# Second layer norm applied behind the adapter product, with a centred adapter: a Hyena block with an adapter on one Trainium2 core

## The reference, cut to what matters

```python
# x: (8, 2048, 512); D_MODEL 512, ORDER 2
def _layernorm(x, eps=1e-5):
    m = mean(x, -1); v = var(x, -1)
    return (x - m) / sqrt(v + eps)

def hyena(x):                                   # only the last branch survives the loop
    proj = (x @ in_proj_w + in_proj_b).reshape(B, L, C, 3)
    v = short_conv3(proj[..., 0]) + short_b
    h = coefs(pos)[:, :, 1]                     # small network over positions
    conv = irfft(rfft(v, n=2 * L) * rfft(h, n=2 * L))[:, :L]
    return (proj[..., 2] * conv) @ out_w + out_b

def adapter(x):                                 # K = 8 chosen of 32 adapters
    out = einsum('k,kod,bsd->bso', weights, W[ids], x)
    return out + einsum('k,ko->o', weights, b[ids])

x = x + hyena(_layernorm(x))
x = x + adapter(_layernorm(x))                  # the layer norm that the change is about
```

## Time and profile before

| | |
|---|---|
| median of 3 runs | 2428.93 us (2424.77, 2428.93, 2429.24) |
| the profiled execution's own time | 2427.41 us |
| its span, first to last instruction | 2425.2 us |
| mean granted TensorE clock | 0.979 |
| TensorE busy, whole span | 2317.4 us, 96% |
| VectorE busy | 1553.6 us, 64% |
| GpSimd busy | 942.7 us, 39% |
| ScalarE busy | 843.5 us, 35% |

### The profile page before, as it was taken

How to read it: one execution, slowest core, us unless ns; L and a number is a source line. 1 busy time by engine, 2 the same in 40 slices (tenths; PEclk the granted TensorE clock), 3 DMA queues, 4 the chain that set the end, 5 groups by cost and what they waited for, 6 DMA issues and landing times. The chain is left out here.

```text
span 2425.2 us, 39710 instructions
## 1 busy us (share of the span) xinstructions
PE 2317.4 (96%) x12804; PEld 1602.1 (66%) x12804; DVE 1553.6 (64%) x2188; ACT 843.5 (35%) x1151; POOL 942.7 (39%) x1189
## 2 busy tenths in 40 slices
PE   6779999999999999779999988999999999999998
PEld 2257777777777777534444435777777777777776
DVE  5834444343434444257777767888888888888886
ACT  3334444444444444334444441222222222222222
POOL 1322222222222222100000006777777777777774
PEclk9879999999999999889999998999999999999999
DMA  5534545445444546489999988766666556665653
GB/s 184 217 100 139 186 165 178 160 154 196 156 160 145 190 153 212 158 337 356 361 355 358 359 315 257 227 182 177 179 177 181 174 175 179 175 176 177 179 179 103
DMA packets 180517, 496.60 MB, mean 205 GB/s; under 512 B 19419, under 2 KB 19740, under 8 KB 159332
## 3 DMA queue, kind: packets, MB, share of 16 engines
q1 hardware_dynamic: 150756, 395.10, 50.7%
q10 hardware_dynamic: 29696, 100.68, 11.5%
HBM read 276.27 MB, written 219.43 MB: 204 GB/s over the span
## 5 line engine op out<-in xcount | busy, mean ns | idle before, releaser
L1055 DVE TENSOR_TENSOR m_m<-m_psA,m_spec 128x1024 f32<-128x1024 f32 x256 | 295.4, 1216 | 132.0 <-PE m_psA L960 128.6
L709 POOL TENSOR_TENSOR vl<-v,vh 128x512 fp32r<-128x512 f32 x128 | 165.2, 1291 | 390.0 <-ACT vh L663 390.0
L1222 ACT ACTIVATE b_zh<-b_psT 128x512 fp32r<-128x512 f32 x128 | 76.5, 597 | 636.8 <-PE b_psT L1271 636.8
L977 PE MATMUL m_psW<-m_m,mats 64*64 64x512 f32 x2048 | 249.6, 593 | 0.0
L960 PE MATMUL m_psA<-m_xin,mats 64*64 64x512 f32 x1536 | 203.9, 602 | 30.5 <-DMA m_xin<-spec_f 13.5
L181 PE MATMUL psV<-wvh,nth 128*128 128x512 f32 x512 | 213.6, 417 | 0.6 <-DVE ntl L791 0.6
L810 DVE TENSOR_TENSOR gto<-psG,bgr 128x512 f32<-128x512 f32 x128 | 87.7, 685 | 195.5 <-PE psG L183 195.4
L181 PE MATMUL b_psO<-woh,b_oh 128*128 128x512 f32 x512 | 211.2, 412 | 0.0
L181 PE MATMUL b_psF<-wfh,b_zh 128*128 128x512 f32 x512 | 207.6, 406 | 2.8 <-DVE b_zl L1324 2.8
L1191 POOL TENSOR_TENSOR b_corr<-b_edge,b_v 128x512 f32<-128x512 f32 x128 | 199.2, 1556 | 14.5 <-DMA b_edge<-edge_f 14.4
L182 PE MATMUL b_psF<-wfl,b_zh 128*128 128x512 f32 x512 | 201.3, 393 | 0.0
(11 more groups left out here) (122 smaller groups left out, 4494.6 us busy)
## 6 DMA issues: line engine op xcount, KB each, us to landing
spec<-fs1o SPq DMA_DIRECT2D x64, 1024.0 KB, 8.8
spec<-m_wo ACTq DMA_DIRECT2D x64, 1024.0 KB, 8.4
b_fin<-spec SPq DMA_DIRECT2D x128, 512.0 KB, 4.6
m_xin<-spec SPq DMA_DIRECT2D x31, 2048.0 KB, 11.8
xg<-in_L_attn_x_dram SPq DMA_DIRECT2D x64, 512.0 KB, 6.1
gate_d<-gto SPq DMA_DIRECT2D x32, 1024.0 KB, 3.9
b_gin<-gate_d SPq DMA_DIRECT2D x128, 256.0 KB, 3.6
b_xin<-in_L_attn_x_dram SPq DMA_DIRECT2D x256, 128.0 KB, 3.2
```

The source lines that it names most:

```text
L709: pool.tensor_tensor(vl[:, t % 2], v[:, t % 2], vh[:, t % 2].bitcast(F32), ALU.subtract).then_inc(v_lo, 1)
L977: mm = pe.matmul(psW[pair % 2][half[slot], q, :], ws[slot][half[q]], m[half[q], pair % RM, part, slot, :], start=part == 0, stop=part == 1)
L1055: dve.tensor_tensor(m[:, (k - 2) % RM, part], psA[k % RA][:], spec[:, par, part], ALU.mult).then_inc(m_done, 1)
```

## The change

The second layer norm is no longer applied to y ahead of the product.

- In `front`, a new VectorE stage `level` takes the mean of each row of the mixed adapter off it, one of four pieces in each of four rounds of the last batch, ahead of the write to HBM. `store_mix` moves from tile 5 to tile 11 of the last batch in SP's list and also waits for `level`.
- In `back`, `norm` is gone, `turn_z` transposes y itself, and `scalars` computes only r (two operations instead of four). `finish` multiplies the product by r and adds `b_yb` in one operation, and waits for r.
- `z_high`, `z_low`, `turn_z`, `adapt`, `finish` and `store` run with a lag one smaller, and on VectorE `finish` stands ahead of `z_low` and `o_low`.

```diff
 (front, SP)
-                    if isinstance(b, int) and b == B - 1 and t == MIX:
+                    if isinstance(b, int) and b == B - 1 and t == T - 5:
                         sp.wait_ge(ad_used, MIX * B)
+                        sp.wait_ge(ad_level, CT)
                         sp.dma_start(ad_mix, ad_sum[:]).then_inc(ad_stored, 16)
                         sp.dma_start(ad_bias, adb_sum[:]).then_inc(ad_stored, 16)
 (front, VectorE)
-                pipelined(dve, B, T, [(nt_low, 3), (v_bias, 4), (moments, 0), (g_bias, 4), (mix, 9)])
+                def level(b, t):
+
+                    if not (isinstance(b, int) and b == B - 1 and MIX <= t < MIX + CT):
+                        return
+                    k = t - MIX
+                    dve.wait_ge(ad_used, MIX * (B - 1) + k + 1)
+                    dve.bn_stats(ad_stats[:, k], ad_sum[:, k]).then_inc(ad_step, 1)
+                    dve.wait_ge(ad_step, 2 * k + 1)
+                    dve.bn_aggr(ad_mean[:, k], ad_stats[:, k]).then_inc(ad_step, 1)
+                    dve.wait_ge(ad_step, 2 * k + 2)
+                    dve.tensor_scalar(ad_sum[:, k], ad_sum[:, k], ad_mean[:, k, 0:1], None, ALU.subtract).then_inc(ad_level, 1)
+
+                pipelined(dve, B, T, [(nt_low, 3), (v_bias, 4), (moments, 0), (g_bias, 4), (mix, 9), (level, 9)])
 (back, GpSimd)
                     if old(b, t, 2):
-                        pool.wait_ge(z_done, no(b, t) - 1)
-                    r, m = rstd[:, t % 2:t % 2 + 1], shift[:, t % 2:t % 2 + 1]
+                        pool.wait_ge(res_done, no(b, t) - 1)
+                    r = rstd[:, t % 2:t % 2 + 1]
                     pool.tensor_tensor(r, mv[:, 1:2], eps[:], ALU.add).then_inc(pow_step, 1)
-                    pool.tensor_tensor(m, mv[:, 0:1], minus[:], ALU.mult).then_inc(pow_step, 1)
-                    pool.wait_ge(pow_step, 3 * no(b, t) + 2)
-                    pool.tensor_tensor(r, r, power[:], ALU.pow).then_inc(pow_step, 1)
-                    pool.wait_ge(pow_step, 3 * no(b, t) + 3)
-                    pool.tensor_tensor(m, m, r, ALU.mult).then_inc(norm_ready, 1)
+                    pool.wait_ge(pow_step, no(b, t) + 1)
+                    pool.tensor_tensor(r, r, power[:], ALU.pow).then_inc(norm_ready, 1)
 (back, ScalarE)
-                def norm(b, t):
-                    ...
-                pipelined(act, B, T, [(z_high, 4), (o_high, 1), (norm, 3), (store, 6)])
+                pipelined(act, B, T, [(z_high, 3), (o_high, 1), (store, 5)])
 (back, TensorE)
                 def turn_z(b, t):
-                    pe.wait_ge(z_done, no(b, t) + 1)
+                    pe.wait_ge(y_done, no(b, t) + 1)
                     if old(b, t, 1):
                         pe.wait_ge(z_lo, no(b, t))
                     for ct in range(CT):
-                        mm = pe.transpose(psT[:, ct * P:(ct + 1) * P], z[:, t % 2, ct * P:(ct + 1) * P], ident[:])
+                        mm = pe.transpose(psT[:, ct * P:(ct + 1) * P], y[:, t % 2, ct * P:(ct + 1) * P], ident[:])
-                pipelined(pe, B, T, [(conv_pair, 0), (adapt, 5), (turn_z, 4), (turn_o, 1), (project, 2)])
+                pipelined(pe, B, T, [(conv_pair, 0), (adapt, 4), (turn_z, 3), (turn_o, 1), (project, 2)])
 (back, VectorE)
-                        dve.wait_ge(z_done, no(b, t) - 1)
+                        dve.wait_ge(t_ps, no(b, t) - 1)
                 def finish(b, t):
                     dve.wait_ge(ff_ps, no(b, t) + 1)
                     dve.wait_ge(yb_done, no(b, t) + 1)
+                    dve.wait_ge(norm_ready, no(b, t) + 1)
-                    dve.tensor_tensor(res[:, t % D], psF[t % 2][:], yb[:, t % D], ALU.add).then_inc(res_done, 1)
+                    dve.scalar_tensor_tensor(res[:, t % D], psF[t % 2][:], rstd[:, t % 2:t % 2 + 1], yb[:, t % D], ALU.mult, ALU.add).then_inc(res_done, 1)
-                pipelined(dve, B, T, [(gate, 1), (residual, 3), (z_low, 4), (o_low, 1), (finish, 5), (bias_x, 0)])
+                pipelined(dve, B, T, [(gate, 1), (residual, 3), (finish, 4), (z_low, 3), (o_low, 1), (bias_x, 0)])
```

More of the change, by code:

```diff
@@ L522, in front @@
             adb_sum = sb("adb_sum", [P, C])
+            ad_stats = sb("ad_stats", [P, CT, 6])
+            ad_mean = sb("ad_mean", [P, CT, 2])
             wgt = sb("wgt", [P, NIDS])
@@ L541, in front @@
             ad_stored = sem("f_ad_stored")
+            ad_step = sem("f_ad_step")
+            ad_level = sem("f_ad_level")
             power_set = sem("f_power_set")
@@ L1084, in back @@
             y = sb("b_y", [P, 2, C])
-            z = sb("b_z", [P, 2, C])
             yb = sb("b_yb", [P, D, C])
@@ L1092, in back @@
             rstd = sb("b_rstd", [P, 2])
-            shift = sb("b_shift", [P, 2])
             power = sb("b_power", [P, 1])
             eps = sb("b_eps", [P, 1])
-            minus = sb("b_minus", [P, 1])
             psC = [ps("b_psC0"), ps("b_psC1")]
@@ L1124, in back @@
             norm_ready = sem("b_norm_ready")
-            z_done = sem("b_z_done")
             yb_done = sem("b_yb_done")
@@ L1167, in _ @@
                 pool.memset(eps[:], EPS).then_inc(power_set, 1)
-                pool.memset(minus[:], -1.0).then_inc(power_set, 1)
-                pool.wait_ge(power_set, 3)
+                pool.wait_ge(power_set, 2)
                 def scalars(b, t):
```

## The result

The changed kernel takes 2447.07 us (median of 4, 2446.04 to 2447.91) against 2426.85 before (median of 4): ratio 1.0088, 95% interval 1.0075 to 1.0101 (the two medians alone give 1.0083). It is some 20 us slower. The forecast was 2426, the range ended at 2440. The profiled execution took 2446.04 us, its span is 2444.2.

The account below looks back on a forecast made before the run. TensorE was taken to bound the back stage, busy 929.74 of 930 us. The terms, 0 steady - 1.7 at the end - 1.1 at the start = -2.8 us from the 2428.93 median, gave 2426 us; range 2422 to 2440.

Parts of the forecast that it names:

- the part on VectorE: Back stage: finish takes 0.06 us more, filling an idle hole; the new wait and 0.74 a round would not bind.
- the steady term of the sum: Back stage's repeated pairs of rounds, 14.81 us each on TensorE: no stall, so 0 us change.
- Does y come in time?: Back stage: y done 5.95 us behind the odd turn, even turn loading at 6.12, so TensorE does not stall.
- Rival 1: Back stage: the y loop outlasts TensorE's pair if GpSimd saves under 0.385 us a round; 2433 to 2439 us, chance 0.20.
- this margin of 0.1 us: Back stage: y's slack ahead of the even turn, 0.17 us, or some 0.12 after the semaphore.
- The saving on GpSimd: Back stage: two of four small operations go, saving 0.41 us a round, bounds 0.28 and 0.5.
- `finish` and the port: Back stage: finish, with one SBUF tensor, stays outside VectorE's port lock with GpSimd and takes a constant 0.68 to 0.74 us.
- Rival 3: Back stage: finish takes the shared port and delays GpSimd; 2451 us, or 2487 if both rounds pay; chance 0.08.
- Front stage: Front stage: level adds 1.8 us in each of four rounds, 7.3 in all, hidden in VectorE's idle time; cost 0.
- The ends: Back stage's ends: one TensorE stand fewer at the end gains 1.7 us, a shorter start gains 1.1.
- The sum of the repaired kernel: Whole kernel: 0 steady, 1.7 and 1.1 us gained at the ends, giving 2426.1 from the median of 2428.93.

Follow-up runs that it names:

- e1: Changed kernel with finish waiting for norm_ready at the last tile alone: 2425.91 us against 2427.6 for the kernel before, ratio 0.9993.
- e2: Changed kernel with 32 semaphore increments more on VectorE ahead of the back stage's loop: 2427.34 us, ratio 1.0001 to the kernel before.
- e7: Changed kernel with an empty stage of lag 5 in VectorE's list, cutting the loop one round later: 2426.48 us, ratio 0.9993 to the kernel before.
- e9: Kernel before with the new front stage alone (level and the later store_mix), its own back stage kept: 2426.74 us, ratio 1.0000.
- e8: Changed kernel with finish waiting at the last tile alone and an empty lag-5 stage on VectorE: 2425.69 us, ratio 0.9993 to the kernel before.
- e3: Kernel before with only the wait for norm_ready added in finish: 2427.73 us, ratio 1.0000.
- e5: Changed kernel with finish waiting at the last tile alone, plus 24 semaphore increments ahead of VectorE's loop: 2449.15 us, ratio 1.0087 to the kernel before.
- e6: Changed kernel with 128 semaphore increments ahead of VectorE's loop: 2451.86 us, ratio 1.0088 to the kernel before.

## Why the prediction was wrong, point by point

**The step that failed** is in the part on VectorE: "The new wait for `norm_ready` is for a value of the round before. If the cover were gone, 0.74 a round on VectorE (83% busy) would still not bind." I costed the wait by whether it would ever have to wait. In the loop it never does, as `bn_aggr` has waited for the same value. Its price is the instruction itself, 14 more in the loop body and 12 ahead of it, and where they put the body's end. The second half of the slip is in the steady term of the sum, put at 0 from one pair of rounds that holds no jump back: the shorter lags took away y's round to spare and moved the jump to a round without a hole. That term measured some 21 us (next paragraph). Without the loads it is 0 even with the shorter lags (e1, e2), and so it is with the loads where the jump stands ahead of an odd round (e7). No rival had any of this; the range left it out.

**What it cost.** Five jumps in the steady loop. The five pairs, by stretch:

```profile
1714.71:1734.44 19.73, 16.61 (x74) 12.23 (x73) 11.48 (x18) 2.22 (x4) 9.70 (x10) 0.91 0.45 133
1838.34:1857.15 18.81, 16.60 (x74) 12.14 (x72) 11.47 (x18) 2.17 (x4) 9.70 (x10) 0.91 0.46 140
1961.10:1979.80 18.70, 16.58 (x74) 12.15 (x73) 11.52 (x18) 2.17 (x4) 9.68 (x10) 0.91 0.45 139
2083.70:2102.60 18.90, 16.61 (x74) 12.15 (x73) 11.53 (x18) 2.17 (x4) 9.71 (x10) 0.91 0.44 137
2206.50:2223.60 17.10, 15.06 (x74) 11.01 (x73) 11.55 (x18) 2.18 (x4) 9.69 (x10) 1.00 0.49 154
```

Together 93.24 us instead of 5 x 14.81 = 74.05: 19.2 us too many. TensorE stands for 93.24 - 81.46 = 11.8 of them, 3.1 us in the first pair and 2.0 to 2.3 in the others. The other 7.4 are matmuls that take longer, nearly all in the four pairs whose mean granted clock is 0.91; the fifth, with a stand of 2.0 us, kept 1.00. The 0.91 is a mix of the two levels: in each of the four pairs, 0.9 to 1.3 us behind the end of the stand, the granted clock falls to 0.50 (1.2 GHz) for 3.4 us, which at half speed is 1.7 us of work lost. The first fall, and the fifth pair behind its stand:

```profile
1725.20:1728.60 3.40, 3.40 (x11) 2.75 (x9) 2.83 (x5) 0.96 (x2) 3.01 (x4) 0.50 0.76 214
...
2215.04:2223.58 8.54, 8.54 (x41) 5.80 (x41) 6.29 (x11) 1.09 (x2) 4.96 (x5) 1.00 0.50 157
```

With 0.8 us for the pairs right behind and about 1 for small delays elsewhere, 21 us are lost and some 3.5 gained at the ends. That is the 17.5 us by which the back stage (first load issued at 1451.97, end 2444.2) is longer than before (1450.45, 2425.2). The front and middle stages make up the rest, 1.5 us, within what executions differ.

**Does y come in time?** Right, to 0.07 us. An undisturbed pair after the change, timelines of TensorE and VectorE, against the earlier trace rows:

```profile
1808.72 0.60 PE L1273 MATMUL b_psT<-b_ident,b_y 128*128 128x128 f32 x4
...
1815.07 0.60 PE L1273 MATMUL b_psT<-b_ident,b_y 128*128 128x128 f32 x4
...
1823.53 0.60 PE L1273 MATMUL b_psT<-b_ident,b_y 128*128 128x128 f32 x4
```
```profile
1814.06 0.68 DVE L1314 TENSOR_TENSOR b_y<-b_psO,b_xin 128x512 f32<-128x512 f32 x1
```

Turn to turn is 6.35 and 14.81 us; y is done 6.02 us behind the odd turn, where 5.95 was forecast and 6.12 was the limit. Rival 1 did not happen. Nor was this margin of 0.1 us what failed: e1 has the same order and lags and is busy 930.00 of 930 us.

**The saving on GpSimd.** Forecast 0.41 a round; `bias_y` 0.77 behind the first operation instead of 1.18. The timeline of GpSimd, against the earlier trace rows:

```profile
1808.57 0.19 POOL L1189 TENSOR_TENSOR b_rstd<-b_mv,b_eps 128x1 f32<-128x1 f32 x1 [2.32 <-DVE b_mv L1322]
1808.83 0.55 POOL L1191 TENSOR_TENSOR b_rstd<-b_rstd,b_power 128x1 f32<-128x1 f32 x1
1809.35 1.29 POOL L1208 TENSOR_TENSOR b_yb<-b_y,bfr 128x512 f32<-128x512 f32 x1
```

It is 0.78, a saving of 0.40.

**`finish` and the port.** Forecast 0.74, constant. The tile b_res, min/median/max in ns, against the earlier trace rows:

```profile
L1334 DVE SCALAR_TENSOR_TENSOR b_res<-b_psF,b_rstd,b_yb x125: 749/750/752, 1484.0 to 2422.9; 128x512 f32<-128x512 f32 x125
```

0.75 in all 125, 0.01 over the upper bound, and it stays so in the 57 that run beside one of GpSimd's operations of 128 x 512. L1189 begins 0.08 us behind the moments in 119 of 125 tiles and 0.16 behind in the other six. Rival 3 is out: with its scalar read from SBUF, `finish` did not stand for GpSimd. (The 2487 of that rival does not follow from its own terms: twice 0.44 us in a loop of 14.76 is 0.83 too long, 63 times which is 52 us, that is 2478. Nothing rests on it.)

**Front stage.** `level` takes 0.68 + 0.18 + 0.49 us of work in 1.43 us and is hidden, shown by e9. The forecast had 1.8 us each, also hidden.

**The ends.** At the end, one stand instead of two: from the turn ahead of the last projection but one to the end of the span are 21.46 us (2422.74 to 2444.2). Before it was 26.28 (2398.92 to 2425.2), with one more product and turn in it, 3.17: gain 1.65, forecast 1.7. At the start the convolution that began 33.75 us behind the first load begins at 35.08, with 3.17 more behind it: 1.8, forecast 1.1. The sum of the repaired kernel was 2426.1 from a median of 2428.93, that is a ratio of 0.9988. e1, e7 and e8 measured 0.9993, with 0.9988 inside each interval; e2 measured 1.0001, and its interval, from 0.9992, leaves 0.9988 out. That the repaired kernel is faster at all is not shown.

## What to carry to other kernels

In a loop with a jump back, a wait that never waits is not always free: it is an instruction, and a few more can shift and lengthen the body until it is loaded anew in each pass (e1 against the changed kernel: 20 us). Look in the DMA view for instruction packets in the steady part, and for "issue" behind the branch; count the body before and after an edit.

A round taken out of a pipeline can also take out the cover for rare things, a jump, a boundary, that no average shows, and it moves the place where the loop is cut. Look for them at the period of the outer loop before shortening, and if a stall can't be removed, cut the loop where the engine waits anyway (e7: one empty stage, 20 us).

## What the runs showed of the hardware that was not expected

- A jump back with loads behind it kept VectorE from its next record for 2.97 to 5.31 us (changed kernel, e3 to e7), one without for 0.21 to 0.23; in the changed kernel three packets of 8 KB fall between 1715 and 1725 us. Whether it happens changes with 24 to 32 instructions of position and repeats after 128 (e2, e5, e6).
- Stands of TensorE of 2.1 to 3.1 us each cost 1.8 us more in the matmuls behind them (granted clock 0.91 over the pair, busy 16.58 to 16.61 instead of 14.81 us). The projection's matmuls of the first such pair average 453 to 510 ns by kind, against 397 to 418 over the whole kernel. A stand of 2.0 us left the clock at 1.00. The length of the stand does not decide by itself: in e5 one of 2.48 us (from 1722.85) left it at 1.00, and one of 2.08 us (from 1844.11) was followed by the fall.
- A VectorE operation with both operands in SBUF that began while one of GpSimd's of 128 x 512 ran ended 0.55 us behind it in the rows that the prediction used, and 0.54 to 0.55 in three cases of the changed kernel (L1291 and L1302 from 1808 to 1819 us). A timetable built on it met y to 0.07 us.
